# An adaptive-norm transformer block on one core: exponentials of the first twelve groups tile by tile, a set-up product in six calls, and a new order of calls

## What is computed

```python
mod = (silu(c) @ wmod).reshape(8, 6, 1, 256)          # sa, ca, ga, sb, cb, gb
h = layernorm(x) * (1 + ca) + sa
hn = layernorm(h) * ln1_w + ln1_b
q, k, v = hn @ Wq + bq, hn @ Wk + bk, hn @ Wv + bv    # 16 heads of width 16
p = softmax(q @ k.T / 4 + band)                       # key j for row i: i - 128 <= j <= i
h = h + (p @ v) @ Wo + bo
h = h + gelu(layernorm2(h) @ W1 + b1) @ W2 + b2
x = x + ga * h
h = layernorm(x) * (1 + cb) + sb                      # h_prev: the row before
r, k = sigmoid(mix_r(h, h_prev) @ W_r.T), mix_k(h, h_prev) @ W_k.T
x = x + gb * (r * (relu(k)**2 @ W_v.T))
```

## Time and profile before

| | before |
|---|---|
| median of 3 runs | 625.58 us (621.79 to 627.44) |
| the profiled execution | 628.59 us |
| its span, first to last instruction | 626.8 us |
| granted TensorE clock, mean | 0.983 |
| PE busy | 572.5 us (91%) |
| ACT busy | 446.6 us (71%) |
| DVE busy | 408.4 us (65%) |
| POOL busy | 360.2 us (57%) |
| DMA | 55.73 MB, mean 89 GB/s |

### The profile page before, as it was taken

The page is one execution under the profiler, slowest core; times in us unless marked ns, Lnnn a source line. Parts: engine busy times, 40 slices in busy tenths (PEclk is TensorE's granted clock), DMA queues, the critical chain, the costliest instruction groups (busy, mean ns, idle before and its releaser), DMA issues.

```text
span 626.8 us, 16500 instructions
## 1 busy us (share of the span) xinstructions
PE 572.5 (91%) x6528; PEld 446.6 (71%) x6528; DVE 408.4 (65%) x847; ACT 446.6 (71%) x745; POOL 360.2 (57%) x594
## 2 busy tenths in 40 slices
PE   5979998899998998999898999899999989999896
PEld 2657767677776776677666776677767768878785
DVE  4588655686475768676866687667856485365553
ACT  2427547399968778796879786987789787965542
POOL 4103323847755958666766758585757377953430
PEclk9889979899999999999999999999999999999999
DMA  5545512613613052351325232443124142110111
GB/s 161 205 133 127 132 42 79 157 47 95 162 41 84 18 138 57 98 135 47 86 75 160 76 87 74 121 116 89 46 76 119 50 113 74 53 46 26 35 43 35
DMA packets 46363, 55.73 MB, mean 89 GB/s; under 512 B 11643, under 2 KB 33469, under 8 KB 46286
## 3 DMA queue, kind: packets, MB, share of 16 engines
q1 hardware_dynamic: 44454, 53.81, 31.0%
q10 hardware_dynamic: 1832, 0.87, 0.6%
HBM read 22.31 MB, written 4.49 MB: 43 GB/s over the span
## 4 chain that ended last, share of the span: by engine, by line
PE 42%; ACT 16%; DVE 16%; issue 7%; POOL 7%; DMA 6%; SPq 5%; ACTq 1%; DVEq 0%; POOLq 0%
DVE nmax L1528 3%; PE rest L484 3%; ACT rest L1046 3%; PE rest L359 3%; PE rest L445 3%; PE rest L496 3%; PE rest L472 3%; PE quad L340 3%; PE rest L447 3%; PE rest L446 3%; PE quad L396 2%; ACT hid_hi L1056 2%; ACT p L995 2%; DMA rb<-den_rows 2%; PE rest L237 2%
## 5 line engine op out<-in xcount | busy, mean ns | idle before, releaser
L2163 POOL TENSOR_SCALAR_AFFINE_SELECT p<-p 128x448 f32<-128x448 f32 x64 | 41.3, 646 | 129.3 <-ACT p L995 106.1
L1528 DVE TENSOR_REDUCE nmax<-quad 128x8 f32<-128x1032 f32 x64 | 78.9, 1233 | 2.2
L428 PE MATMUL rest<-bt_hi,w_hi 128*128 128x256 f16 x256 | 70.2, 274 | 5.3 <-DVE hid_lo L1588 5.1
L995 ACT ACTIVATE p<-quad,scale_s 128x576 f32<-128x576 f32 (+1 forms) x77 | 62.2, 821 | 16.4 <-PE quad L340 16.3
L1046 ACT ACTIVATE rest<-rest,bias,scale_g 128x256 f32<-128x256 f32 x128 | 62.9, 532 | 11.2 <-PE rest L430 11.0
L445 PE MATMUL rest<-w_hi,hid_hi 128*128 128x256 f16 x256 | 69.9, 273 | 0.8 <-DVE hid_lo L1588 0.8
L430 PE MATMUL rest<-bt_hi,w_lo 128*128 128x256 f16 x256 | 69.8, 273 | 0.0
L429 PE MATMUL rest<-bt_lo,w_hi 128*128 128x256 f16 x256 | 69.8, 273 | 0.0
L447 PE MATMUL rest<-w_hi,hid_lo 128*128 128x256 f16 x256 | 69.8, 273 | 0.0
L446 PE MATMUL rest<-w_lo,hid_hi 128*128 128x256 f16 x256 | 69.8, 272 | 0.0
L1588 DVE SCALAR_TENSOR_TENSOR hid_lo<-rest,inv_f,hid_hi 128x512 f16<-128x512 f32 x64 | 46.8, 744 | 24.9 <-ACT hid_hi L1056 24.6
(11 more groups left out here) (231 smaller groups left out, 1523.4 us busy)
## 6 DMA issues: line engine op xcount, KB each, us to landing
k_st<-k_two SPq DMA_DIRECT2D x64, 128.0 KB, 2.5
v_blk<-vn SPq DMA_DIRECT2D x16, 512.0 KB, 6.4
q_st<-q_two SPq DMA_DIRECT2D x64, 64.0 KB, 2.6
k_st<-k_two SPq DMA_DIRECT2D x64, 64.0 KB, 2.0
rb<-den_rows SPq DMA_DIRECT2D x16, 256.0 KB
x<-x SPq DMA_DIRECT2D x16, 256.0 KB, 2.8
out<-x SPq DMA_DIRECT2D x16, 256.0 KB, 2.2
xa<-x SPq DMA_DIRECT2D x7, 512.0 KB, 4.6
```

What stands on the lines that cost most here:

```text
L428: e.matmul(dst, w1_hi[:, k, ms], bt_hi[:, k, :], start=(k == 0), stop=False)
L995: e.activation(p32[gp % SLOTS][:, c0:c0 + 2 * w].rearrange("p (n c) -> p n c", n=2), (rest if gp < APART else quad)[:, b0 % HQ:b0 % HQ + 2 ...
L1528: e.tensor_reduce(nmax[:, :, :, qt].rearrange("p a j -> p j a"), quad[:, :, 2 * QB - 2:2 * WIN].rearrange("p j (c a) -> p j a c", a=2), AX ...
```

## The change

1. **Exponentials.** For the groups below `APART`, `exps` issues one ACTIVATE per tile instead of one per two tiles, and each raises the semaphore `s_ex`, so that a bank is free as soon as its tile is read. `ex_count` gives the new counts to `scores`, `select` and three waits that stood for "all twelve groups". Later groups keep their pairs.
2. **Set-up product.** `setup_attn` on PE is six calls of two matmuls instead of one of twelve. The six calls stand in a row, so PE's instructions there are the same.
3. **Order.** All five lists of calls are written in another order, from the start through the loop to the end. The numbers of calls are the same; only the 24 ACTIVATEs of edit 1 come on top. Several calls cross the border between the start list and the loop, so that a turn of a loop begins at another place.

```diff
+        def ex_count(gp, i):
+            return 4 * gp + i + 1 if gp < APART else 2 * APART + 2 * gp + i // 2 + 1
...
                 if n == WARM + 5:
-                    e.wait_ge(s_ex, 2 * APART)
+                    e.wait_ge(s_ex, 4 * APART)
...
-                    bank, free = ring_q[gp].take(("st", gp, i), s_ex, 2 * gp + i // 2 + 1)
+                    bank, free = ring_q[gp].take(("st", gp, i), s_ex, ex_count(gp, i))
...
-            def setup_attn():
-                e.wait_ge(s_col, DMA)
-                e.wait_ge(s_wa, DMA)
-                for m in range(6):
-                    for k in range(KC):
+            def setup_attn(m):
+                if m == 0:
+                    e.wait_ge(s_col, DMA)
+                    e.wait_ge(s_wa, DMA)
+                for k in range(KC):
...
+                if gp < APART:
+                    for i in range(first, last_):
+                        w, c0 = EW2[i], sum(EW2[0:i])
+                        e.wait_ge(s_st, 4 * gp + i + 1)
+                        e.activation(p32[gp % SLOTS][:, c0:c0 + w], ring_q[gp].at["st", gp, i][:, 0:w], ACT.Exp,
+                                     scale=scale_s[:, 1:2]).then_inc(s_ex, 1)
+                    return
...
             max_rows(0)
+            project(1)
             values(0, 0)
             values(0, 1)
-            project(1)
             scores(0, 0, 2)
...
-                e.wait_ge(s_ex, 2 * (gp + 1))
+                e.wait_ge(s_ex, ex_count(gp, 3))
...
                 save_den(u - 1)
                 spread_den(u - 1)
+                store(u - 5)
                 load_v(b)
-                store(u - 5)
                 stacks(u + 1, 0, 2)
                 load_residual(u - 3)
+                stacks(u + 1, 2, 4)
                 fold_den(u)
```

More of the change, by code:

```diff
@@ L767, in _ @@
             transposes_d(1)
-            for b in range(3, 7):
+            values(3, 1)
+            scores(23, 0, 2)
+            down(2, 0)
+            maxima(6, 3)
+            keys(1)
+            scores(23, 2, 4)
+            transposes_b(3)
+            for b in range(3, 6):
                 u = 2 * b
                 gp = 8 * b
-                scores(gp - 1, 0, 2)
-                values(b, 1)
-                down(u - 4, 0)
-                maxima(u, 3)
-                keys(u - 5)
-                transposes_b(u - 3)
                 max_rows(u)
-                scores(gp - 1, 2, 4)
                 project(u + 1)
@@ L1276, in _ @@
             exps(22, 2, 4)
[L1277 removed]
             gelu(2, 0, 2)
+            high_f(2, 0, 1)
+            gelu(2, 2, 4)
             norm_c(1)
[L1280 to L1282 removed]
             high_f(2, 1, 2)
@@ L1288, in _ @@
             modulate(1)
+            copy_v(3, 1)
+            exps(23, 0, 2)
             for b in range(3, 7):
@@ new lines, in _ @@
+            for b in range(2, 5):
+                u = 2 * b
+                mix(u - 3)
+                maxima(u + 2, 3)
+                low_m(u + 2)
+                scale_c(u)
+                low_qk(u + 3)
+                scale_x(b + 2)
+                low_b(u - 1)
+                shift_x(b + 2)
+                divide(u + 1)
+                add_y(u - 2)
+                stats_h(b + 2)
+                gated(u - 3)
+                maxima(u + 3, 0)
+                low_f(u - 1, 0, 1)
+                scale_c(u + 1)
+                low_f(u - 1, 1, 2)
+                maxima(u + 3, 1)
+                output(u - 3)
+                residual_b(u - 2)
+                residual_a(u)
+                low_f(u - 1, 2, 3)
+                low_f(u - 1, 3, 4)
+                maxima(u + 3, 2)
+                stats_b(u)
+                low_a(b + 2)
+                mix(u - 2)
+                maxima(u + 3, 3)
+                low_m(u + 3)
+                add_y(u - 1)
+                low_qk(u + 4)
+                residual_b(u - 1)
+                low_b(u)
+                maxima(u + 4, 0)
+                maxima(u + 4, 1)
+                low_f(u, 0, 1)
+                low_f(u, 1, 2)
+                residual_a(u + 1)
+                stats_b(u + 1)
+                divide(u + 2)
+                gated(u - 2)
+                maxima(u + 4, 2)
+                output(u - 2)
+                stats_x(b + 3)
+                low_f(u, 2, 3)
+                low_f(u, 3, 4)
@@ L1987, in _ @@
+            mix(7)
+            maxima(NU - 4, 3)
+            low_m(NU - 4)
+            scale_c(10)
             low_qk(NU - 3)
```

716 lines of the change are left out of this document (362 added, 354 removed).

## The result

| | before | changed |
|---|---|---|
| median | 625.8 us (621.8 to 627.4, 6 runs) | 632.1 us (630.3 to 635.2, 6 runs) |
| ratio | | 1.0124, 95% interval 1.0087 to 1.0160 |
| the profiled execution | 628.59 us | 635.19 us |
| its span | 626.8 us | 633.4 us |
| granted clock, mean | 0.983 | 0.982 |

What follows compares the result with a forecast made beforehand. PE was taken to bound the loop, a chain of hand-overs between engines the start. From the profiled 628.59 us, 6.0 (start) and 1.2 (loop) gave 621.4; 3.0 us lower for the median, 618.4 us, range 609 to 629.

Steps and rivals of the forecast that it cites:

- the stop of DVE behind `load_v(1)`: Before `maxima(3, 3)`: DVE's `scale_c(1)` was expected to stop some 2 us, with `max_rows(3)` and `out_project(0)` behind it.
- Up to `max_rows(0)`: Start: less `warm` ahead of `transposes_a(0)` and an earlier `scale_x(1)`; net gain 0.7 us, bounds 0.9 loss to 2.5 gain.
- the 1.1 us of `warm` moved and the 0.88 us wait removed: Up to `max_rows(0)`: `transposes_a(0)` no longer behind nine `warm` matmuls; `scale_x(1)` no longer waiting for the modulation rows.
- To `transposes_a(1)`: Start: `project(1)` ahead of batch 0's values gives 1.7 us more, 2.4 us in all; bounds 0.7 and 3.4.
- To `context(0)` and `context(1)`: Start: earlier `load_x(2)`, then reordered splitting of pass 3; gain in all 3.1 us, then 4.6 us.
- To `context(2)`: Start: shorter PE waits through edit 1, less a DVE stop; net 1.4 us more, 6.0 in all, bounds 2 and 9.
- Edit 1: First 115 us: 3.4 us more ACT work off the path; PE's 3.7 us of bank waits 1.8 us shorter.
- The loop: Each turn: `low_m` ahead of DVE's 1.54 us denominators' stop; 0.3 us for four turns, 1.2 us, bounds 0 and 6.2.
- The rival of late values: Loop: `load_v` behind `store` makes values late, 2 to 3 us in each of four turns; 634 us, chance 13%.
- The end: Last 100 us: swaps of neighbours only, costed at nothing, with 1 us either way.
- the rival of a gain given back: Behind `context(2)`: ACT or slower-clocked PE takes back the start's gain, 0 to 3 us remain; about 624 us, chance 29%.
- the third: Rival for the loop: values arrive late in each turn, and the start wins nothing; 634 us, chance 13%.

Runs made afterwards that it cites:

- b2: The kernel before, unchanged, profiled a second time; `context(2)` came at 120.39 us instead of 123.43.
- m2: Kernel before with one move on SP, `load_v(1)` ahead of `spread_den(1)` and `load_x(3)`; ratio 1.0097 to before.
- e1: Changed kernel with `load_v(1)` back behind `spread_den(1)` and `load_x(3)` on SP; 628.6 us, ratio 1.0074 to before.
- e4: Kernel before with edit 1 alone (first twelve groups' exponentials tile by tile); ratio 0.9990 to before.
- e5: Changed kernel with edit 1 undone (exponentials in pairs again), order kept; 636.4 us, ratio 1.0188 to before.
- h5: Kernel before plus edit 1, with the changed order only inside the loop; ratio 0.9994 to before.
- n1: Changed kernel with `load_v(1)` and `load_w2` moved back, plus `residual_b(12)` ahead of `divide(15)`, `scale_c(15)` ahead of `output(11)`; `context(15)` to end 79.02 us, 79.81 without the last two.

## Why the prediction was wrong

**The step that failed.** The forecast was 7.2 us under before, the result 6.3 us over it. Of these 13.5 us, 8.0 are the start: 6.0 us of gain forecast at `context(2)`, 2.0 of loss measured. Another 4.7 are stretches that I costed at nothing: 2.9 up to `context(6)` and 1.8 at the end. The rest is the loop. In the start the term mis-sized most is the stop of DVE behind `load_v(1)`, put at 2 us.

**The base of the sum.** I subtracted 6.0 us from an execution of 628.59 us that lay 3.0 us over the median, and took those 3.0 us off again at the end. By itself that moved the forecast by nothing: it is the median less 7.2 us. But the 3.0 us stood where I looked for the gain: b2 has all of them before `context(2)`, 1.0 by `project(0)`, where both profiles have a fall of the clock, 0.6 more by `max_rows(0)` and the others behind. The marks of before held them, and a mark of the changed kernel that comes earlier than these by less than 3 us shows no gain by itself.

**Up to `max_rows(0)`, 0.7 us: wrong.** From `project(0)` it takes 16.6 us in all profiles with the new order of the start, and 16.0 to 17.0 with the old. `scale_x(1)` ran at 27.72 us without a wait, as said; the 1.1 us of `warm` moved and the 0.88 us wait removed were not worth anything that the profiles show. Without the early fall `project(0)` comes at 24.4 to 24.9 us with the new order and at 24.0 to 24.5 with the old: `transposes_a(0)`, now ahead of `warm`, waits 1.8 us for POOL there. Of the 2.9 us by which the mark came earlier, 2.5 were there at `project(0)`, and go with the early fall that this profile lacks.

**To `transposes_a(1)`, 2.4 us: wrong in sign.** It came at 64.19 instead of 63.48 us. I gave every DMA on SP a place, but not the small one in ACT's queue: `max_send(0)` now met 1 MB of `load_w2`, which I had not priced as an obstacle to anything. PE stood 2.44 us, and 44 to 63 us ran at 0.82.

**To `context(0)` and `context(1)`, 3.1 and 4.6 us: not earned.** They came at 79.39 and 96.26 us, 0.4 and 1.8 us earlier, less than the 2.5 us of `project(0)`; in b2 they stand at 78.16 and 95.94 us.

**To `context(2)`, 6.0 us: wrong; this term failed most.** `context(2)` came at 125.69 us, 2.3 us later than in the earlier trace rows, where the forecast had 117.5. The mechanism was right, `load_v(1)` ahead of `spread_den(1)`, DVE stopped before `maxima(3, 3)`, but its size was 5.37 us, not 2: c1 to c2 took 29.4 us. A fall of the clock overlapped with it; in the changed kernel it began ahead of PE's stop, in m2 (at about 115.8 us) within it, so what share is the clock's is not shown. e1 and m2 price the order at 3.1 and 6.1 us of the end. I had taken the landing of 1 MB of values as a delay that `rb` shares in part; in fact `rb` was used 9.3 us after its issue. The Trainium skill, "DMA: Bandwidth & Descriptors", section "Queues, rings and completion order", says that the descriptors of one queue are consumed in ring order on each DMA engine; the trace agrees, since with the two issues swapped the same DMA was used after 4.3 us.

**Edit 1: right in its price.** 3.4 us more ACT, off the path, and PE's direct waits 3.7 to 2.0 us, where I had said 1.9. That the 1.8 us of shorter waits are won at the end is not shown (e4: 0.9990, 0.9957 to 1.0024). The rule of the Trainium skill, "ScalarE: Activation LUTs", section "Rules for kernel authors", that I had weighed (an estimate of 7.2 us), was twice too dear here, by ACT's busy time of e5 and the changed kernel.

**The loop, 1.2 us: wrong, 0.3 to 0.4 in the profiles, nothing by the times of h5.** DVE's stop of 1.54 us for the denominators is gone, but between 260 and 328 us DVE waits 7.9 us in three pieces for ACT's `m_t` instead, since `low_m` stands first now. The rival of late values did not come: SP's `store` went out at 379.81 instead of 381.52 us, the values right behind it at 380.30, and `context(10)` waited for neither.

**The end, 0 with 1 us either way: wrong, 1.8 us lost**, and `context(2)` to `context(6)`, which I had not costed at all, lost 2.9. The end I took for swaps of neighbours, and for the stretch behind `context(2)` I had only the rival of a gain given back. n1 shows what one such swap is: a call that waits for a DMA put ahead of one on the path. Which calls make the 2.9 us stays open.

The rival nearest to the outcome was the third, 634 us, but that is luck: the late values that it is made of did not come.

## What to carry to other kernels

When a large transfer moves earlier, price it by the small DMAs behind it that someone waits for, in the other queue too. Here the one issued 1.3 us behind the values was used 5.0 us later than with the order swapped; the one in ACT's queue, 3.0 us behind 1 MB, was late by some 2.4 us, which the times at the end don't show. Before a gain is summed from marks, take a second profile of the same kernel: what differs between the two is not the order's. A swap of neighbours can't be costed at nothing if the one that now goes first waits for something: one such swap and its partner were worth 0.8 us in n1.

## What the runs showed of the hardware

The two profiles of the kernel before agree within 0.3 us in every distance between contexts from `context(2)` to the end, 503.4 and 503.5 us, and differ by 3.0 us before it: 1.0 by `project(0)` and 2.0 behind, where the clock of 80 to 98 and 98 to 124 us is 0.82 and 0.93 in one and 0.89 and 1.00 in the other. Over all profiles the granted clock fell to half at 14 to 22 us with PE busy all the time (4.00 of 4.00 us), in or right behind 24 matmuls of one column, in 9 of 16. In those nine the four matmuls ahead of these had taken 2.3 to 3.0 us instead of 1.9. The Trainium skill, "TensorE: Matmul & The Clock Gate", Part 1, makes the clock depend on how busy PE has been; here busy time alone does not tell it, in the records at least.

The user of a 16 KB DMA in ACT's queue started 6.1 us after its issue, behind 1 MB issued on SP 3.0 us before it. (With that load moved back no wait for it is left in seven profiles.) Behind the two DMAs of the values even SP's issue of the next took 1.87 us (1.95 in m2) instead of 0.64 in e1.
